# Router logits in four column groups, and class scores' products in rounds, in a ViT layer on one core

## The chip, the cores and the metric

One core of a Trainium2 chip runs the program in one launch. The metric is the device time of one execution in microseconds. The profile is of one execution; the median is of three others.

## What is computed

The input has 16 images of 512 tokens, 256 wide. The layer mixes tokens with a gated product, puts a class token ahead of each image (513 rows), adds a 16-head attention with quantized projections, and adds a mixture of 8 experts of which each token takes 2. Cut to what matters here:

```python
scores = jnp.einsum('bhqd,bhkd->bhqk', q, k) * SCALE      # 513 x 513 per head, 16 heads
attn = jax.nn.softmax(scores, axis=-1)
...
router_logits = x_flat @ gate_w                            # x_flat: layernorm(h), 8208 x 256; gate_w: 256 x 8
router_probs = jax.nn.softmax(router_logits, axis=-1)
top_k_probs, top_k_idx = jax.lax.top_k(router_probs, 2)
```

The class token's row and column of the scores are computed apart from the 512 x 512 rest: these are the "class scores". The router logits choose the experts of each token. Both are fp32 products.

## The kernel before

The token phase goes over the images in steps. One step works on five images at once, each in another stage: T (token mixing), P (projections and quantization, one image back), C (attention, the first groups of heads), W (attention, the last ones, and its output), X (output projection, second norm, router). So X's image is two behind C's, and in the last two of the 16 steps of X there is no C. Three steps ahead of the loop and the last ones are written out; between them a hardware loop runs two images a lap.

A step has 64 units (`at`), 4 groups of 16 (`u`). The order is written out by hand, for each engine in its own program, and engines meet at semaphores. In each unit:

- PE makes one tile of scores (L503) for VectorE and, with the row maximum taken in, one transposed tile (L512) for ScalarE. L503 may be only two tiles ahead of VectorE (`dve_mx`), L512 only two ahead of ScalarE (`act_exp`).
- VectorE takes the row maximum (`head_max`, L1183) at the head of the unit, then the unit's other work.
- ScalarE does the unit's other work first and `exps` (L833) last.
- Every fourth unit PE multiplies by the values (L521), four heads at once in four column groups: each product writes 32 of the bank's 128 partitions, from stationary tiles of 32 columns.

Every fp32 product with a moving tile other than a transposition shows as two records. Bank `d2` is shared in turn by many small jobs; each waits until the one before has been read.

What stands around the change, all for image X unless said:

- Unit 3 (image C): the class scores, L604 to L610. Eight products of 32 stationary and 256 moving columns, into four column groups of `d2`: for each of two operand pairs and two halves, the two slices `c` of the contraction.
- Units 28 and 30: PE transposes the normed x2 (L721); ScalarE copies it to `x2_t` in units 29 and 31 (L928).
- Unit 33: `logits` (L784 to L792). For each of four token blocks and two slices, a block of x2_t (128 columns) is the stationary operand and the 8 columns of gate_w move. The result is 128 tokens x 4 blocks x 8 experts in `d2`.
- Unit 34: VectorE copies it to `lg` (L1263), and the router goes on in units 35, 37, 41. ScalarE's unit 33 copies part_kh (L935), which waits for VectorE's fk of unit 32; unit 34 copies part_qm (L938), which releases POOL's part_ql (L1054) and then its rest (L1059).
- Unit 34 of PE also has the token product L552 (image T), unit 35 the class token's values (L748, image W) into `d2` after `dve_lg`; ScalarE's unit 36 copies pvs (L846); unit 38 of PE transposes it (L645).

A copy of `logits` serves the class tokens after the loop (L814 on). SP loads gate_w in setup (L376). The expert phase after that has nothing of the change.

Of the kernel before, what the change touches and what calls it, by code (L numbers as in the profile page):

```python
# [8 lines left out]
ACT = mybir.ActivationFunctionType  # L9
# [8 lines left out]
E, F = 8, 512  # L18
EPS = 1e-5
TB = S // 128  # L20
# [130 lines left out]
def token_phase(nc, outer, images, x_t, cls, w0_t, w1_t, wo_t, attn_w_t, gate_w, consts, out,  # L151
# [19 lines left out]

    gate_sb = keep("gate_sb", [128, DC, E])
    ones_bf = keep("ones_bf", [128, 128], BF16)
# [193 lines left out]
    def sync_program(sp, stage):  # L367
        if stage == SETUP:
            sp.dma_start(cst[:, :], consts).then_inc(s("cst_in"), 16)
            sp.dma_start(w_stage.rearrange("p (w c n) -> p w c n", w=4, c=DC),  # L370
                         attn_w_t.rearrange("w (c p) n -> p w c n", p=128)).then_inc(s("attn_w_in"), 16)
            sp.dma_start(cls_row[:, :], cls).then_inc(s("cls_in"), 16)
            sp.dma_start(w0[:, :, :], w0_t.rearrange("(c p) n -> p c n", p=128)).then_inc(s("tok_w_in"), 16)
            sp.dma_start(w1[:, :, :], w1_t.rearrange("(c p) n -> p c n", p=128)).then_inc(s("tok_w_in"), 16)
            sp.dma_start(wo[:, :, :], wo_t.rearrange("(c p) n -> p c n", p=128)).then_inc(s("tok_w_in"), 16)
            sp.dma_start(gate_sb[:, :, :], gate_w.rearrange("(c p) n -> p c n", p=128)).then_inc(s("gate_in"), 16)  # L376

# [97 lines left out]
    def tensor_program(pe, stage):  # L475
# [49 lines left out]
        def body(T, P, C, W, X):  # L525
            for g in range(NG):
                for u in range(UNITS):
# [73 lines left out]
                    if C.ok and at == 3:  # L601

                        wait(pe, s("dve_bd"), 2, C, 2)
                        wait(pe, s("act_vc"), 1, C, 1)  # L604
                        for k, (a, o) in enumerate(((fq, kbd), (fk, qbd))):
                            for half in range(2):
                                for c in range(DC):
                                    last = mm(d2[VW * (2 * k + half):VW * (2 * k + half + 1), 0:S // 2], o[:, c, :],
                                              a[:, c, half * S // 2:(half + 1) * S // 2], start=(c == 0), stop=(c == DC - 1))
                        last.then_inc(s("pe_ct"), 1)  # L610
# [99 lines left out]
                    if X.ok and at in (28, 30):  # L710
# [9 lines left out]
                        for t in range(TB):  # L720
                            last = tr(d2[:, blk(t)], x2[:, t, blk(c)], identf)  # L721
                        last.then_inc(s("pe_x2t"), 1)
                    if X.ok and at == 33:
                        logits(X, TB, 128, "", [])
                    if P.ok and at in (41, 42):
# [58 lines left out]
        def logits(b, nt, np_, x, free):  # L784
# [3 lines left out]
            for t in range(nt):  # L788
                for c in range(DC):
                    last = mm(d2[0:np_, t * E:(t + 1) * E], x2_t[:, c, t * 128:t * 128 + np_], gate_sb[:, c, :],  # L790
                              start=(c == 0), stop=(c == DC - 1))
# [29 lines left out]
    def scalar_program(act, stage):  # L821
# [13 lines left out]
        def body(T, P, C, W, X):  # L835
            for g in range(NG):
                for u in range(UNITS):
# [86 lines left out]
                    if X.ok and at in (29, 31):  # L924
                        c = (at - 29) // 2
                        wait(act, s("pe_x2t"), DC, X, c + 1)
                        wait(act, s("pe_lg"), 1, X, 0)
                        f(x2_t[:, c, :], d2[:, :], ACT.Copy).then_inc(s("act_x2t"), 1)  # L928
                    if P.ok and at == 29:
                        wait(act, s("dve_fq"), DC, P, DC)  # L930
# [165 lines left out]
    def vector_program(dve, stage):  # L1096
# [30 lines left out]
        one = At(0)  # L1127
        if stage == SETUP:
            v.memset(ones[:, :], 1.0).then_inc(s("ones_set"), 1)
            v.memset(am2[:, :], 1.0).then_inc(s("ones_set"), 1)  # L1130
# [122 lines left out]
        def router(b, x, nt, np_, pieces=(0, 1, 2, 3)):  # L1253
# [4 lines left out]
            for piece in pieces:  # L1258
                k = piece // 2
                ch = Link("dve_chain_r" + x, 10, b, (0, 2, 5, 7)[piece])  # L1260
                if piece == 0:
                    wait(dve, s("pe_lg" + x), 1, b, 1)
                    signal(v.tensor_copy(lg[P, 0:nt, :], d2[P, 0:nt * E].rearrange("p (t e) -> p t e", e=E)),  # L1263
                           "dve_lg" + x, 1, b, 1)
                if piece == 2:
# [671 lines left out]
```

## Time and profile before

| | us |
|---|---|
| median of 3 runs | 2311.74 |
| the runs | 2311.74, 2303.79, 2311.91 |
| the profiled execution | 2304.04 |
| its span, first to last instruction | 2302.2 |
| PE busy in the span | 2008.1 (87%) |
| VectorE busy | 1532.5 (67%) |
| ScalarE busy | 1266.3 (55%) |
| POOL busy | 924.0 (40%) |

"Busy" of PE is the time in which some matmul record is open; records of neighbouring matmuls overlap, since their ends are modelled. PEld is the weight load, beside PE. "Idle before" names how long the engine had done nothing ahead of an instruction, and the instruction that ended the wait. The token phase takes about the first 1650 us. In the loop an image takes 91 to 97 us.

### The profile page before, as it was taken

The page shows a single profiled execution, that of the slowest core. Times are in us where ns is not written, and L with a number is a line of the kernel's source. Part 1 is how long each engine was busy: PE and PEld are TensorE (multiplying, and loading weights), DVE is VectorE, ACT ScalarE, POOL GpSimd, SP SyncE. Part 2 cuts the span into 40 slices and gives each one's busy share as a digit, 9 for nine tenths or more (in the row PEclk, how much of TensorE's full clock was granted, in tenths as well). Part 3 has the DMA queues.
Part 4 walks back from the last instruction along what each step waited for, and adds up shares of the span by engine and source line. Part 5 has one row for each costly group of instructions (what it writes and reads, how often), then busy time and mean ns, then how long its engine had stood idle before and what let it go on. Part 6 is the DMA issues. An engine that isn't in the chain of part 4 may idle for free. (4 is left out here: it accounts for less than half of the span.)

```text
span 2302.2 us, 49649 instructions
## 1 busy us (share of the span) xinstructions
PE 2008.1 (87%) x13312; PEld 1151.8 (50%) x13329; DVE 1532.5 (67%) x4076; ACT 1266.3 (55%) x2792; POOL 924.0 (40%) x958
## 2 busy tenths in 40 slices
PE   4799999999998998989999998883139999999997
PEld 2343444443444444444344443321038898888885
DVE  4477887877877787788787888873264444444443
ACT  0246666665665665656566567662144555544553
POOL 2222233423433244233342343332236666666653
PEclk9799999999999999999899999996569999999999
DMA  2412322322232223233232322310244443333341
GB/s 85 105 56 70 95 76 78 90 79 73 84 79 85 77 68 97 67 84 87 59 97 67 89 75 79 79 43 28 96 162 66 65 64 62 61 62 62 63 59 22
DMA packets 171885, 172.29 MB, mean 75 GB/s; under 512 B 30786, under 2 KB 160404, under 8 KB 171668
## 3 DMA queue, kind: packets, MB, share of 16 engines
q1 hardware_dynamic: 141396, 134.87, 20.4%
q0 software_dynamic: 30272, 34.80, 9.5%
q8 instruction: 103, 1.69, 0.3%
q14 instruction: 114, 0.93, 0.2%
HBM read 100.70 MB, written 68.99 MB: 74 GB/s over the span
## 5 line engine op out<-in xcount | busy, mean ns | idle before, releaser
L1183 DVE TENSOR_REDUCE mxs<-bank 128x1 f32<-128x512 f32 x1024 | 698.6, 686 | 251.2 <-PE bank L503 239.4
L833 ACT ACTIVATE pt<-bank 128x512 f32<-128x512 f32 x1024 | 586.1, 592 | 277.0 <-PE bank L512 272.3
L503 PE MATMUL bank<-ks,qs 96*128 96x512 bf16 x1024 | 399.1, 391 | 72.0 <-DVE mxs L1183 53.9
L512 PE MATMUL bank<-qs,ks 99*128 99x512 bf16 x1024 | 394.7, 387 | 4.4 <-ACT pt L833 3.8
L1792 PE MATMUL bank<-xh,gu_h 128*128 128x256 bf16 (+1 forms) x1152 | 308.9, 268 | 3.8 <-issue 1.9
L1792 PE MATMUL bank<-xl,gu_h 128*128 128x256 bf16 (+1 forms) x1152 | 307.7, 267 | 0.0
L1792 PE MATMUL bank<-xh,gu_l 128*128 128x256 bf16 (+1 forms) x1152 | 307.7, 267 | 0.0
L1752 POOL DMA_INDIRECT out<-y_sb,ids x136 | 217.2, 1597 | 202.1 <-ACT y_sb L1843 177.6
L521 PE MATMUL bank<-pt,v_sb 128*32 128x512 f32 x2048 | 278.9, 617 | 0.0
L503 PEld LDWEIGHTS bank<-ks,qs 96*128 96x128 bf16 x1024 | 104.1, 102 | 338.8 <-DVE mxs L1183 212.5
L1900 DVE TENSOR_TENSOR hid_e<-bank,act_g 128x256 f32<-128x256 f32 (+1 forms) x288 | 117.1, 407 | 169.0 <-PE bank L1792 159.0
L1005 POOL DMA_INDIRECT list_dram<-pay,slot_i x130 | 138.3, 1064 | 227.0 <-DVE pay L1306 192.8
L1904 DVE TENSOR_TENSOR hl<-hid_e,hh 128x256 bf16<-128x256 f32 (+1 forms) x288 | 119.4, 415 | 143.9 <-ACT hh L1857 143.9
L1857 ACT ACTIVATE hh<-hid_e 128x256 bf16<-128x256 f32 (+1 forms) x288 | 116.5, 405 | 163.8 <-DVE hid_e L1900 163.8
L1022 POOL TENSOR_TENSOR cadd<-vcls,pr 128x256 f32<-128x256 f32 x64 | 40.9, 639 | 372.4 <-DVE pr L1228 372.1
L1742 POOL DMA_INDIRECT xg<-x_dram,ids x136 | 137.1, 1008 | 62.9 <-issue 41.2
L1803 PE MATMUL bank<-dn_h,hh 128*128 x544 | 148.5, 273 | 3.5 <-ACT hh L1857 3.5
L1803 PE MATMUL bank<-dn_h,hl 128*128 x544 | 148.3, 273 | 0.0
L1803 PE MATMUL bank<-dn_l,hh 128*128 x544 | 148.3, 273 | 0.0
L512 PEld LDWEIGHTS bank<-qs,ks 99*128 99x128 bf16 x1024 | 100.2, 98 | 90.7 <-issue 38.0
L552 PE MATMUL bank<-xt,w 128*128 128x512 f32 x256 | 130.6, 634 | 8.1 <-DMA xt<-x_t 8.0
L572 PE MATMUL bank<-wo,hid 128*128 128x256 f32 x512 | 124.1, 388 | 4.2 <-ACT v_sb L952 3.4
(290 smaller groups left out, 3432.1 us busy)
## 6 DMA issues: line engine op xcount, KB each, us to landing
qs<-qk_dram SPq DMA_DIRECT2D x128, 128.0 KB, 2.6
ks<-qk_dram SPq DMA_DIRECT2D x64, 192.0 KB, 3.3
xt<-x_t SPq DMA_DIRECT2D x16, 512.0 KB, 4.4
h_dram<-h_sb SPq DMA_DIRECT2D x16, 512.0 KB, 4.1
qs<-qk_dram SPq DMA_DIRECT2D x128, 64.0 KB, 2.2
ks<-qk_dram SPq DMA_DIRECT2D x64, 128.0 KB, 3.3
hw<-h_dram SPq DMA_DIRECT2D x16, 512.0 KB, 4.1
out<-hw SPq DMA_DIRECT2D x16, 512.0 KB, 3.0
```

The costliest lines, as they stand in the source:

```text
L503: mm(score[u % 2][:, :], qs[0:QK, h, blk(t)], ks[0:QK, h, :], start=True, stop=True) \
L512: mm(scoret[u % 2][:, :], ks[0:QK + MROWS, h, blk(t)], qs[0:QK + MROWS, h, :], start=True, stop=True).then_inc(s("pe_st"), 1)
L521: last = mm(pv_bank[VW * j:VW * (j + 1), :], v_sb[:, b.par, t, g * GH + j, :], pt[:, t % 2, j, :], start=(t == 0), stop=(t == TB - 1))
L552: last = mm(d0[:, :], w0[:, c, blk(e)], xt[:, T.par, c, :], start=(c == 0), stop=(c == DC - 1))
L572: last = mm((d0, d1)[t // 2][:, D * (t % 2):D * (t % 2 + 1)], hid[:, e, blk(t)], wo[:, e, :], start=(e == 0), stop=(e == EC - 1))
L833: f(pt[:, t % 2, j, :], scoret[u % 2][:, :], ACT.Exp).then_inc(s("act_exp"), 1)
L1005: g_.indirect_dma_start(out=list_dram, out_offset=bass.IndirectOffsetOnAxis(ap=slot_i[0:np_, k, t:t + 1], axis=0), in_=pay[0:np_, k, t, :] ...
L1183: v.reduce_max(mxs[:, t, g * GH + j:g * GH + j + 1], score[u % 2][:, :], AX.X).then_inc(s("dve_mx"), 1)
L1742: nc.gpsimd.indirect_dma_start(out=xg[:, i.place(ROWS), b, :], out_offset=None, in_=x2_dram, in_offset=rows(i, b)) \
L1752: nc.gpsimd.indirect_dma_start(out=out, out_offset=rows(i, b), in_=y_sb[:, i.place(2), b, :], in_offset=None, bounds_check=tokens - 1, oob ...
L1792: last = mm(bank[:, 0:n], w[:, bass.ds(e, 1), c, lo:lo + 128], a[:, k, c, 0:n], start=(m == 1), stop=(m == 3 * DC))
L1803: last = mm(y_b[b][:, 0:D], a[:, c, blk(b)], w[:, bass.ds(e, 1), c, :], start=(c == 0 and m == 0), stop=(c == FC - 1 and m == 2))
```

## The change

The class scores' eight products are issued in another order: the slice `c` outermost, so that four products to four column groups follow one another. The router logits of the 16 images are made the other way round: gate_w, padded to 32 columns with zeros, is stationary, the token block moves, and each token block has its own column group; they move to unit 32. They come out transposed (32 padded experts x 4 blocks by 128 tokens), so ScalarE copies them to a new tile `lgt` in its unit 32, PE transposes that in unit 33, and VectorE reads the result from the second quarter of `d2`. The zeros are set by VectorE in setup, and SP's load of gate_w waits for them.

```diff
-    gate_sb = keep("gate_sb", [128, DC, E])
+    gate_sb = keep("gate_sb", [128, DC, VW])
+    lgt = keep("lgt", [128, 128])
...
-            sp.dma_start(gate_sb[:, :, :], gate_w.rearrange("(c p) n -> p c n", p=128)).then_inc(s("gate_in"), 16)
+            sp.wait_ge(s("gate_set"), 1)
+            sp.dma_start(gate_sb[:, :, 0:E], gate_w.rearrange("(c p) n -> p c n", p=128)).then_inc(s("gate_in"), 16)
...
-                        for k, (a, o) in enumerate(((fq, kbd), (fk, qbd))):
-                            for half in range(2):
-                                for c in range(DC):
+                        for c in range(DC):
+                            for k, (a, o) in enumerate(((fq, kbd), (fk, qbd))):
+                                for half in range(2):
                                     last = mm(d2[VW * (2 * k + half):VW * (2 * k + half + 1), 0:S // 2], o[:, c, :],
                                               a[:, c, half * S // 2:(half + 1) * S // 2], start=(c == 0), stop=(c == DC - 1))
...
+                    if X.ok and at == 32:
+                        wait(pe, s("act_x2t"), DC, X, DC)
+                        for c in range(DC):
+                            for t in range(TB):
+                                last = mm(d2[VW * t:VW * (t + 1), 0:128], gate_sb[:, c, :], x2_t[:, c, blk(t)],
+                                          start=(c == 0), stop=(c == DC - 1))
+                        last.then_inc(s("pe_lgt"), 1)
                     if X.ok and at == 33:
-                        logits(X, TB, 128, "", [])
+                        wait(pe, s("act_lgt"), 1, X, 1)
+                        tr(d2[:, 128:256], lgt[:, :], identf).then_inc(s("pe_lg"), 1)
...
-                    last = mm(d2[0:np_, t * E:(t + 1) * E], x2_t[:, c, t * 128:t * 128 + np_], gate_sb[:, c, :],
+                    last = mm(d2[0:np_, t * E:(t + 1) * E], x2_t[:, c, t * 128:t * 128 + np_], gate_sb[:, c, 0:E],
...
+                    if X.ok and at == 32:
+                        wait(act, s("pe_lgt"), 1, X, 1)
+                        wait(act, s("pe_lg"), 1, X, 0)
+                        f(lgt[:, :], d2[:, 0:128], ACT.Copy).then_inc(s("act_lgt"), 1)
...
+            v.memset(gate_sb[:, :, :], 0.0).then_inc(s("gate_set"), 1)
...
-                    signal(v.tensor_copy(lg[P, 0:nt, :], d2[P, 0:nt * E].rearrange("p (t e) -> p t e", e=E)),
-                           "dve_lg" + x, 1, b, 1)
+                    got = d2[P, 0:nt * E].rearrange("p (t e) -> p t e", e=E) if x else \
+                        d2[:, 128:256].rearrange("p (t w) -> p t w", w=VW)[:, :, 0:E]
+                    signal(v.tensor_copy(lg[P, 0:nt, :], got), "dve_lg" + x, 1, b, 1)
```

## Rows read from the trace of the kernel before

**Rows 1.** The profile page, its head.

```profile
span 2302.2 us, 49649 instructions
```

**Rows 2.** Stretch between two logits: its length, busy us of PE, PEld, DVE, ACT, POOL.

```profile
968.71:1061.40 92.69, 85.79 (x482) 38.56 (x483) 74.31 (x203) 57.81 (x124) 34.02 (x42) 0.98 0.28 77
```

**Rows 3.** Timeline of PE, units 32 to 34: start us, length us, engine, line.

```profile
966.35 0.38 PE L512 MATMUL bank<-qs,ks 99*128 99x512 bf16 x1
966.57 0.38 PE L503 MATMUL bank<-ks,qs 96*128 96x512 bf16 x1
...
967.00 1.85 PE L790 MATMUL bank<-gate_sb,x_t 128*128 128x8 f32 x16
968.71 0.38 PE L503 MATMUL bank<-ks,qs 96*128 96x512 bf16 x1
...
969.14 0.59 PE L552 MATMUL bank<-xt,w 128*128 128x512 f32 x1
```

**Rows 4.** Groups by line: busy us, mean ns; of L895 min/median/max ns.

```profile
L790 PEld LDWEIGHTS bank<-gate_sb,x_t 128*128 128x128 f32 x260 | 32.8, 199 | 4.4 <-ACT x_t L928 1.9 <-ACT x_t L976 0.4
L608 PEld LDWEIGHTS bank<-fq,kbd 128*32 128x32 f32 x128 | 8.0, 116 | 14.8 <-DVE qbd L1357 11.2 <-issue 2.1
L645 PEld LDWEIGHTS bank<-cst,pvs 128*128 128x128 f32 x256 | 31.8, 141 | 11.9 <-issue 1.7
...
L895 ACT ACTIVATE sct<-bank x16: 372/381/391, 107.3 to 1474.4; 128x256 f32<-128x256 f32 x16
```

**Rows 5.** Timelines of ACT, then of DVE, units 31 to 37.

```profile
964.85 0.59 ACT L928 ACTIVATE x_t<-bank 128x512 f32<-128x512 f32 x1
...
966.85 0.60 ACT L833 ACTIVATE pt<-bank 128x512 f32<-128x512 f32 x1
967.93 1.06 ACT L935 ACTIVATE part_kh<-fk 128x1024 bf16<-128x1024 f32 x1 [0.48 <-DVE fk L1450]
...
972.60 0.60 ACT L846 ACTIVATE pvs<-bank 128x512 f32<-128x512 f32 x1 [0.28 <-PE bank L521]
...
969.12 0.69 DVE L1183 TENSOR_REDUCE mxs<-bank 128x1 f32<-128x512 f32 x1 [0.46 <-PE bank L503]
...
976.58 0.69 DVE L1183 TENSOR_REDUCE mxs<-bank 128x1 f32<-128x512 f32 x1 [1.00 <-PE bank L503]
```

**Rows 6.** Timeline of PE at the class scores of the same step, unit 3.

```profile
924.99 0.41 PE L608 MATMUL bank<-fq,kbd 128*32 128x256 f32 x2
925.00 0.42 PE L608 MATMUL bank<-fk,qbd 128*32 128x256 f32 x2
925.20 0.41 PE L608 MATMUL bank<-fq,kbd 128*32 128x256 f32 x2
...
925.68 0.39 PE L608 MATMUL bank<-fk,qbd 128*32 128x256 f32 x2
926.00 0.39 PE L503 MATMUL bank<-ks,qs 96*128 96x512 bf16 x1
```

**Rows 7.** Timeline of PE at the products with the values, unit 35.

```profile
971.08 0.38 PE L512 MATMUL bank<-qs,ks 99*128 99x512 bf16 x1
971.38 1.06 PE L521 MATMUL bank<-pt,v_sb 128*32 128x512 f32 x8
```

**Rows 8.** Timeline of PE and DVE, units 38 to 40.

```profile
977.03 0.60 PE L645 MATMUL bank<-cst,pvs 128*128 128x128 f32 x4
977.47 0.38 PE L503 MATMUL bank<-ks,qs 96*128 96x512 bf16 x1
...
979.21 0.68 DVE L1183 TENSOR_REDUCE mxs<-bank 128x1 f32<-128x512 f32 x1
...
979.95 0.39 PE L503 MATMUL bank<-ks,qs 96*128 96x512 bf16 x1 [0.35 <-DVE mxs L1183]
```

**Rows 9.** Timeline of POOL, the first work behind its chain of part_ql and rest.

```profile
981.76 0.63 POOL L1022 TENSOR_TENSOR cadd<-vcls,pr 128x256 f32<-128x256 f32 x1 [6.33 <-DVE pr L1228]
```

**Rows 10.** Timeline of PE in the last image's step.

```profile
1615.06 3.58 PE L790 MATMUL bank<-gate_sb,x_t 128*128 128x8 f32 x16 [0.69 <-ACT x_t L928]
```

## The prediction

> **What bounds the kernel now.** I read the page's head first, then the table of stages, then stretches in order of time. The span is 2302.2 us [rows 1]; the profiled execution took 2304.04 us, so 1.8 us lie around the span. A whole stretch from one image's logits to the next shows PE busy 85.79 of 92.69 us (93%), VectorE 80%, ScalarE 62% [rows 2]. PE is the engine to relieve. It is not the only limit: in some units it waits for VectorE's maxima, as at 979.95 [rows 8]. So I ask of each saving whether PE sets the end where it falls, and what comes next.
>
> The old logits (L790) are a plain stop of PE. From their first product at 967.00 to the next scores (L503) at 968.71 pass 1.71 us [rows 3]. Weight loads fill them: 16 loads of 128 fp32 columns, 199 ns each and overlapping by half (260 in all: 16 for each of 16 images, 4 in the class-token stage) [rows 4], against products of 8 columns. In 14 of the 16 steps another image's scores stand beside them (that image is two ahead). Meanwhile VectorE waits: 0.46 us before the maximum at 969.12 and 1.00 before that at 976.58, both for L503 [rows 5]. The first wait of PE behind the logits is the 0.35 us at 979.95 [rows 8]. Hence VectorE follows PE here, and time saved at the logits starts everything behind it earlier.
>
> **The class scores' order costs or gives nearly nothing.** The edit only changes the order of 8 products (16 records, since each is two passes). The four column groups already run side by side: records of both pairs start at 924.99 and 925.00, the next round at 925.20 [rows 6]. The last round ends its starts at 925.68 and the next scores start at 926.00, so 1.01 us in all, against 4 rounds of 0.21 = 0.85 plus the way out. Rounds in the program can remove only the stagger inside a round, about 0.02 us: 16 x 0.02 = 0.3 us. Bounds: 0 and 1.01 - 0.85 = 0.16 us an image.
>
> [...]
>
> **The logits, step by step**, on the clock of [rows 3] (the old start is 967.00).
> 1. In unit 32 the L512 product starts at 966.35 and its neighbour 0.22 later, so PE is free at 966.57. Entering column groups costs 0.09 us: L521 starts 0.30 after L512 at 971.38, where 0.21 is usual [rows 7]. First logit product: 966.66. The wait for x2_t is over: its second copy ended at 965.44 [rows 5] (964.85 + 0.59).
> 2. Eight fp32 products in four groups are 16 records, 4 rounds. A round of 256 columns takes 0.21 us [rows 6]; 128 columns I take at half, 0.107. End 967.09. The way out costs 0.11 (925.68 + 0.21 to 926.00) [rows 6], so unit 33's L503 starts at 967.20, L512 at 967.42, PE free at 967.63.
> 3. ScalarE's new copy waits for those products. Its nearest relation: L846 starts at 972.60, 0.16 after the modelled end of the L521 group, 971.38 + 1.06 [rows 5, 7]. The new group's modelled end is its last start 966.98 + 0.27 = 967.25 (L608's records last 0.17 longer than their round). Copy starts at 967.41. Copies of 256 and 512 columns last 381 and about 600 ns [rows 4, 5]; 128 columns: 0.27 us. End 967.68.
> 4. PE's transposition waits for it, 0.06 us after (L503 starts at 979.95 after the maximum that ended at 979.21 + 0.68) [rows 8]. Four transpositions take 977.03 to 977.47, 0.11 each [rows 8]; a weight load not made ahead adds up to 0.14 (141 ns) [rows 4]. PE free at 967.99, after a stall of 0.11 + 0.14.
> 5. exps(32) is queued behind the copy on ScalarE: it ran at 966.85, now at 967.66 to 968.26. PE's scoret of unit 34 needs it: L512 at 968.32 instead of 968.21. The token product L552 then starts at 968.54 instead of 969.14 [rows 3].
>
> Saving: **0.60 us an image**. Bounds: 1.71 - 0.09 - 0.43 - 0.11 - 0.11 = 0.97 if copy and weight load hide; 0.60 - 0.45 = 0.15 if each round also waits for its loads (0.11 each, L608's load records [rows 4]). No trace row shows 128-column rounds, so both ends stay.
>
> [...]
>
> **Who is behind the new waits.** Behind ScalarE's copy stand exps(32), the copy of part_kh, exps(33), part_qm and relu. part_kh waited for VectorE's fk until 967.93 anyway [rows 5], so this queue runs about 0.3 us later up to exps(35), at 972.0. PE needs exps(34) only in unit 36, over 2 us later, and pvs waited 0.28 us for PE until 972.60 before [rows 5]: the delay ends there. POOL's part_ql, released by part_qm, moves 0.3 us later, but POOL is idle 6.33 us behind that chain [rows 9]. VectorE's router copy (L1263) at 969.73 waits for the transposition, ready at about 968.2 and so covered by the maximum before it. SP gets one wait in setup, on VectorE's first instruction; PE waits there for other loads and weights: 0. The added memset: 0.
>
> From unit 36 on nothing crosses the saving: the waits of [rows 8] are VectorE's own work since its last wait for PE (976.58), which starts earlier as well. They stay as long as they were. So 14 x 0.60 = 8.4 us.
>
> **The last image** runs its logits alone, at the lower clock level: L790 lasts 3.58 us from 1615.06, and VectorE has nothing else to do [rows 10]. The new chain: 4 rounds at twice the time 0.86, ScalarE 0.29 + 0.27, transposition 0.06 + 0.28, way to VectorE 0.2 = 1.96 us; gain 1.6. The image before it has PE waiting for ScalarE's exps at several places; I take 0. The class-token stage keeps its old products (0).
>
> Sum: 8.4 + 1.6 + 0.3 = 10.3, rounded to 10 us: 2304.0 - 10 = 2294.0 on the profiled execution's scale. The median shown is 2311.7, 7.7 us above that execution, two runs near 2311.8 and one at 2303.8. Shifted by that, the forecast is **2301.7 us**, a gain of 0.43%. About 0.5%, 11.5 us, is what a measurement of this kernel can tell from no change.
>
> **Rivals.**
> - Everything hidden. For it: ScalarE is idle 0.48 us before part_kh, and PE could keep loading ahead. Against: PE's unit 33 holds just 0.43 us of work between the products and the transposition, the copy chain 0.65. Price 0.97 x 14 + 1.6 + 0.3 = 15.5 us: 2296 us. Chance 0.17.
> - Rounds wait for their loads. For it: 16 loads and 16 products now stand against 0.43 us of streaming, where L608 has 0.85. Price 0.15 x 14 + 1 = 3 us: 2309 us. Chance 0.16.
> - Slower: **the four groups don't overlap** on short products. Place: unit 32. All 16 records one after another take 16 x 0.107 = 1.71 us, as long as the old ones, and entry, exit, stall (0.25) and transposition (0.11) come on top; exps(32) is 1.3 us later again and holds PE's unit 34 by 0.1 to 0.3 more. Together about +0.8 us x 14 = +11: 2323 us. It decides once a round takes above 0.107 + 0.60/4 = 0.26 us. Against it: L608 groups overlap wholly [rows 6]. Chance 0.12.
> - The class scores gain more: if a group's second record could not start before its first and held up the other groups, the old order would take 4 groups x 3 rounds x 0.21 + 0.21 = 2.7 us, and the new one 1.0: 1.7 x 14 = 24 us more, 2278 us. The measured 1.01 excludes it [rows 6]; chance under 0.01, counted in the first rival.
> - That the change does nothing (column groups not used) is the same as the slower case.
>
> **How the numbers follow.** Forecast case 0.55: range 7 to 13 us of gain, 2298.7 to 2304.7; 0.17 of it lies beyond 11.5 us. Faster by over 0.5%: 0.17 + 0.17 = 0.34. Slower by over 0.5%: 0.10 of the slower rival's 0.12. Within: 0.56. The range goes from the full relief with the median sitting 5 us lower than I shifted it, 2291, to the small gain with 2 us for the unknown bound, 2311. It leaves out the slower rival and some edges, under 0.2.
>
> **What would show it.** Right: L608 from first record to next L503 stays 1.0 us; the new products fill about 0.43 us in unit 32; L512 of unit 32 to L552 of unit 34 is about 2.2 us (was 2.79); a short PE stall before the transposition; L833 at unit 32 about 0.8 us later; VectorE's idle at 969.12 shrinks; the time between logits of neighbouring images falls by 0.6 us. Wrong: a round over 0.2 us, a stall over 0.5 us before the transposition, or step lengths that don't follow, because a wait between 976 and the next logits grew.

## The result, and the profile after

| | before | changed |
|---|---|---|
| median of 6 runs each, us | 2305.5 (2302.1 to 2311.9) | 2290.65 (2285.2 to 2295.9) |
| ratio of the two, with its 95% interval | | 0.9927 (0.9904 to 0.995) |
| profiled execution, us | 2304.04 | 2290.1 |

The medians differ by 14.9 us, where 10 was forecast; the ratio of the comparison gives 0.73%. The changed kernel's 2290.65 us lie 0.35 us below the range and 11.05 us below the forecast of 2301.7. On the profiled executions the gain is 13.9 us. Medians here and below leave out two executions of the kernel before, which took 3231 and 5119 us.

The head of the page and its first table, changed kernel:

```profile
span 2288.3 us, 49749 instructions
...
PE 1996.3 (87%) x13344; PEld 1124.2 (49%) x13345; DVE 1526.2 (67%) x4077; ACT 1265.1 (55%) x2808; POOL 926.0 (40%) x958
```

PE's busy time falls by 11.8 us and ScalarE's is the same in spite of 16 new copies. Now the stretch between two logits that answers to [rows 2], from the same score of one image to that of the next (length, then busy us of PE, PEld, VectorE, ScalarE, POOL; the granted clock is the third from the end):

```profile
961.24:1053.21 91.97, 85.50 (x503) 37.53 (x499) 75.36 (x209) 58.83 (x125) 34.14 (x42) 1.00 0.28 82
```

It is 0.72 us shorter. Units 32 to 34 of that image on PE, to be laid beside [rows 3]:

```profile
960.35 0.38 PE L514 MATMUL bank<-qs,ks 99*128 99x512 bf16 x1
960.66 0.64 PE L729 MATMUL bank<-x_t,gate_sb 128*32 128x128 f32 x16
961.24 0.39 PE L505 MATMUL bank<-ks,qs 96*128 96x512 bf16 x1
961.47 0.38 PE L514 MATMUL bank<-qs,ks 99*128 99x512 bf16 x1
961.78 0.33 PE L734 MATMUL bank<-cst,lgt 128*128 128x128 f32 x1
961.95 0.38 PE L505 MATMUL bank<-ks,qs 96*128 96x512 bf16 x1
962.30 0.39 PE L514 MATMUL bank<-qs,ks 99*128 99x512 bf16 x1
962.52 1.53 PE L554 MATMUL bank<-xt,w 128*128 128x512 f32 x3
```

L729 are the new products and L734 the transposition; the other lines are those of before, moved down by two (L503 is L505, L512 is L514, L521 is L523, L552 is L554). From the transposed scores ("scoret", L514) of unit 32 to the token product of unit 34 are 2.17 us, where 2.79 were. ScalarE and VectorE beside it, for [rows 5] (L942 is the new copy, L843 the exps, L949 the copy of part_kh, L1198 the maximum):

```profile
961.45 0.28 ACT L942 ACTIVATE lgt<-bank 128x128 f32<-128x128 f32 x1 [0.68 <-PE bank L729]
961.64 0.60 ACT L843 ACTIVATE pt<-bank 128x512 f32<-128x512 f32 x1
962.14 1.05 ACT L949 ACTIVATE part_kh<-fk 128x1024 bf16<-128x1024 f32 x1
...
962.59 0.68 DVE L1198 TENSOR_REDUCE mxs<-bank 128x1 f32<-128x512 f32 x1
```

ScalarE's idle time before part_kh is gone, and the maximum after the logits no longer waits for PE (0.46 us before).

**Where the time went.** Read from the starts of PE's scores, the 14 images of each profile in which the loop's order holds (C's images 2 to 15) split into stretches. Each row of this table is the sum of one stretch over these images, worked out as the difference of the starts of two scores, so the columns add up to the span (the row 62 to the next image's 5 holds that image's class scores). The last two columns are the ranges over four profiles of each kind: before, again_before, rounds_only and one_more_memset; after, again_after, joint_after and logits_only.

| stretch (units) | before | changed | difference | kind of before | kind with the logits |
|---|---|---|---|---|---|
| start, to unit 28 of image 2 | 303.1 | 303.6 | +0.5 | 302.4 to 307.1 | 303.2 to 304.0 |
| 28 to 36, the logits | 177.4 | 170.1 | -7.3 | 177.4 to 177.4 | 169.9 to 170.4 |
| 36 to 41 | 80.3 | 80.3 | 0.0 | 80.3 to 80.3 | 80.3 to 80.3 |
| 41 to 46 | 99.8 | 99.1 | -0.7 | 99.8 to 103.2 | 99.1 to 102.0 |
| 46 to 48 | 57.4 | 52.9 | -4.5 | 52.9 to 58.7 | 52.9 to 56.2 |
| 48 to 62 | 234.0 | 232.4 | -1.6 | 232.5 to 234.0 | 232.4 to 233.6 |
| 62 to the next image's 5 | 141.9 | 143.0 | +1.1 | 141.9 to 146.0 | 140.0 to 148.0 |
| 5 to 28 | 427.0 | 426.6 | -0.4 | 426.6 to 427.0 | 425.8 to 427.6 |
| end, from unit 48 of image 15 | 781.2 | 780.3 | -0.9 | 781.2 to 784.3 | 780.3 to 781.6 |

Only the second row lies apart in all profiles of the two kinds, and it holds what was forecast: 7.3 us for 8.4. The saving is not the same in every image: 0.54 us in images 3 to 12 (0.38 in one of them), 0.72 in images 2 and 13, 0.67 in image 15, and in image 14 the stretch is 0.09 longer. The next largest term, 4.5 us in units 46 to 48, is one that the forecast did not have. Four rows (41 to 46, 46 to 48, 48 to 62, and the lap's end, 62 to 5) take several values in one and the same kernel; the lap's end moves most, by 8 us between profiles of the kind with the logits. The means of the four profiles of each kind differ by 13.4 us: 7.3 for the logits, 2.2 in units 46 to 48, 1.5 in units 41 to 46, 1.6 at the end, the rest small.

**Units 46 to 48.** Before, PE there, image 9 (L572 is the output projection):

```profile
988.26 0.61 PE L503 MATMUL bank<-ks,qs 96*128 96x512 bf16 x1 [0.58 <-DVE mxs L1183]
988.66 0.63 PE L512 MATMUL bank<-qs,ks 99*128 99x512 bf16 x1
989.09 3.19 PE L572 MATMUL bank<-wo,hid 128*128 128x256 f32 x8
```

and in the changed kernel:

```profile
981.50 0.39 PE L505 MATMUL bank<-ks,qs 96*128 96x512 bf16 x1 [0.58 <-DVE mxs L1198]
981.73 0.38 PE L514 MATMUL bank<-qs,ks 99*128 99x512 bf16 x1
981.95 1.89 PE L574 MATMUL bank<-wo,hid 128*128 128x256 f32 x8
```

The same products behind the same wait, at another clock. The stretches of 5 us say so; the third number from the end is the granted clock. Before:

```profile
985.00:990.00 5.00, 3.52 (x17) 2.05 (x18) 4.42 (x12) 2.17 (x4) 0.53 (x1) 0.83 0.53 167
```

Changed:

```profile
977.00:982.00 5.00, 3.23 (x23) 1.20 (x20) 4.81 (x10) 2.54 (x6) 2.00 (x2) 1.00 0.39 116
```

Such a spell of the lower clock (granted clock 0.50 from 988.3 to 991.5 us) costs 1.6 us here (5.5 where 3.9 is usual). The profile of before has it at images 7 and 9, and one of 1.3 us at image 14; that of the changed kernel has none in these units. Another one of before, also in image 14 (granted clock 0.66 in the stretch from 1455 to 1460 us), is 1.3 of the 1.6 us in the row 48 to 62.

**Units 41 to 46.** Six units in which VectorE makes the last part of the router. Most even images take 6.6 us there; odd ones 6.6 or 8.3 before, 6.6 or 8.1 after. VectorE in an image with 8.3, before, and beside it POOL, which follows its L1022 of [rows 9] with L1026:

```profile
981.78 0.66 DVE L1275 SCALAR_TENSOR_TENSOR rtmp<-rtmp,cst 128x32 f32<-128x32 f32 x1
982.47 0.19 DVE L1276 TENSOR_REDUCE ix<-rtmp 128x4 f32<-128x32 f32 x1
982.69 0.65 DVE L1277 TENSOR_TENSOR oh<-cst,ix 128x32 f32<-128x32 f32 x1
983.38 1.08 DVE L1280 TENSOR_TENSOR picked<-oh 128x32 bf16<-128x32 f32 x1
...
984.99 0.56 DVE L1289 TENSOR_SCALAR wts<-e21e 128x4 f32<-128x4 f32 x1
...
982.57 0.73 POOL L1026 TENSOR_TENSOR o_sb<-o_sb,cadd 128x256 f32<-128x256 f32 x1 [0.18 <-POOL cadd L1022]
```

and the three with two inputs in an image with 6.6, before:

```profile
415.23 0.18 DVE L1275 SCALAR_TENSOR_TENSOR rtmp<-rtmp,cst 128x32 f32<-128x32 f32 x1
...
415.67 0.29 DVE L1277 TENSOR_TENSOR oh<-cst,ix 128x32 f32<-128x32 f32 x1
415.99 0.19 DVE L1280 TENSOR_TENSOR picked<-oh 128x32 bf16<-128x32 f32 x1
```

The three with two SBUF inputs take two to six times as long. Of those with one input the reduction L1276 keeps its 0.19 us, but L1289 takes 0.56 where it takes 0.16 in the short image. The slow ones don't just run slower: each ends 0.03 to 0.05 us after the POOL operation beside it. L1275 ends at 982.44 and POOL's L1022 at 982.39, L1277 at 983.35 and L1026 at 983.30, and L1280 and L1289 end so behind the two L1064 that follow. So a slow one seems to wait POOL's operation out; the traces show the ends, the cause is not tested. Of the five odd images between the third and the eleventh, three are long in the profile of before, three in that of the changed kernel, four in again_after and joint_after, five in again_before, rounds_only, one_more_memset and logits_only. The second difference, 8.3 against 8.1, is a wait of VectorE for its own L1290, which the trace of before has five times (us, times), though it holds PE only in the three long images:

```profile
L1291 DVE TENSOR_TENSOR wts<-e21e,wts x13: 161/604/848, 327.3 to 1442.4; 128x4 f32<-128x4 f32 x13
...
  DVE wts L1290: 1.4, 5
```

In the changed kernel the same instruction (L1307) has no such line.

**The last image**, for [rows 10]:

```profile
1603.64 1.08 PE L729 MATMUL bank<-x_t,gate_sb 128*32 128x128 f32 x16 [0.69 <-ACT x_t L938]
...
1604.79 0.28 ACT L942 ACTIVATE lgt<-bank 128x128 f32<-128x128 f32 x1 [1.20 <-PE bank L729]
...
1605.12 0.48 PE L734 MATMUL bank<-cst,lgt 128*128 128x128 f32 x1 [0.40 <-ACT lgt L942]
1605.63 0.19 DVE L1280 COPY lg<-bank 128x32 f32<-128x32 f32 x1 [7.75 <-PE bank L734]
```

PE's 16 records take 1.08 us for 3.58 before, both at a granted clock of 0.50.

**The class scores**, for [rows 6]: rounds now stand evenly, and the whole is 0.04 us shorter (0.98 from the first record to the next scores, for 1.01).

```profile
919.04 0.39 PE L610 MATMUL bank<-fq,kbd 128*32 128x256 f32 x2
919.05 0.39 PE L610 MATMUL bank<-fk,qbd 128*32 128x256 f32 x2
919.26 0.39 PE L610 MATMUL bank<-fq,kbd 128*32 128x256 f32 x2
...
920.02 0.39 PE L505 MATMUL bank<-ks,qs 96*128 96x512 bf16 x1
```

### The profile page after: what moved, and what is told of

It is laid out like the page before. It is cut to its first block and busy times, and to the rows that moved or that the text cites. A ratio compares the mean times of both kernels' runs of the same rounds, so it can differ in the third digit from the quotient of the medians.

```text
span 2288.3 us, 49749 instructions
## 1 busy us (share of the span) xinstructions
PE 1996.3 (87%) x13344; PEld 1124.2 (49%) x13345; DVE 1526.2 (67%) x4077; ACT 1265.1 (55%) x2808; POOL 926.0 (40%) x958
## 5 line engine op out<-in xcount | busy, mean ns | idle before, releaser
L1198 DVE TENSOR_REDUCE mxs<-bank 128x1 f32<-128x512 f32 x1024 | 698.0, 685 | 245.3 <-PE bank L505 233.9
L843 ACT ACTIVATE pt<-bank 128x512 f32<-128x512 f32 x1024 | 586.7, 593 | 264.4 <-PE bank L514 260.4
L505 PE MATMUL bank<-ks,qs 96*128 96x512 bf16 x1024 | 397.6, 389 | 72.1 <-DVE mxs L1198 54.1
L514 PE MATMUL bank<-qs,ks 99*128 99x512 bf16 x1024 | 393.9, 386 | 5.7 <-ACT pt L843 5.1
L1808 PE MATMUL bank<-xh,gu_h 128*128 128x256 bf16 (+1 forms) x1152 | 309.4, 269 | 3.6 <-issue 2.0
L1808 PE MATMUL bank<-xl,gu_h 128*128 128x256 bf16 (+1 forms) x1152 | 308.2, 268 | 0.0
L1808 PE MATMUL bank<-xh,gu_l 128*128 128x256 bf16 (+1 forms) x1152 | 308.1, 267 | 0.0
L523 PE MATMUL bank<-pt,v_sb 128*32 128x512 f32 x2048 | 278.7, 617 | 0.0
L505 PEld LDWEIGHTS bank<-ks,qs 96*128 96x128 bf16 x1024 | 103.1, 101 | 340.0 <-DVE mxs L1198 218.3
L514 PEld LDWEIGHTS bank<-qs,ks 99*128 99x128 bf16 x1024 | 100.2, 98 | 95.6 <-issue 39.0
L554 PE MATMUL bank<-xt,w 128*128 128x512 f32 x256 | 130.4, 633 | 8.4 <-DMA xt<-x_t 7.9
```

Of the source, the lines that this page charges most:

```text
L505: mm(score[u % 2][:, :], qs[0:QK, h, blk(t)], ks[0:QK, h, :], start=True, stop=True) \
L514: mm(scoret[u % 2][:, :], ks[0:QK + MROWS, h, blk(t)], qs[0:QK + MROWS, h, :], start=True, stop=True).then_inc(s("pe_st"), 1)
L523: last = mm(pv_bank[VW * j:VW * (j + 1), :], v_sb[:, b.par, t, g * GH + j, :], pt[:, t % 2, j, :], start=(t == 0), stop=(t == TB - 1))
L554: last = mm(d0[:, :], w0[:, c, blk(e)], xt[:, T.par, c, :], start=(c == 0), stop=(c == DC - 1))
L843: f(pt[:, t % 2, j, :], scoret[u % 2][:, :], ACT.Exp).then_inc(s("act_exp"), 1)
L1198: v.reduce_max(mxs[:, t, g * GH + j:g * GH + j + 1], score[u % 2][:, :], AX.X).then_inc(s("dve_mx"), 1)
```

## The experiments

Each ratio is to runs of the kernel before on the same chip, with its 95% interval. "28 to 36" is the length of that stretch, from score to score, in most images of the loop: 12.99 us before, 12.44 changed. Some images of a profile take 0.15 more.

### Which part of the change carries it

**rounds_only**: the kernel before with the class scores' loops in the new order, nothing else.

```diff
-                        for k, (a, o) in enumerate(((fq, kbd), (fk, qbd))):
-                            for half in range(2):
-                                for c in range(DC):
+                        for c in range(DC):
+                            for k, (a, o) in enumerate(((fq, kbd), (fk, qbd))):
+                                for half in range(2):
```

> The kernel before with the class scores' products in rounds, logits as before. Theory A: from the first class score record to the next scores 0.979 us instead of 1.016, so 0.04 us x 14 = 0.5 us, no difference that can be measured: ratio 1.000. Rival: the order gives a part of the 4.6 us by which the gain of 14.9 us exceeds the 10.3 forecast; then this kernel is 3 to 5 us faster than the kernel before.

Measured: 2309.5 us, ratio 0.9997 (0.9984 to 1.0011); 28 to 36 is 12.99. **logits_only**: the changed kernel with the class scores' old order, the same lines turned back.

> The changed kernel with the class scores' old order. Theory A: all of the gain is here: ratio 0.993 to 0.994, 2290 to 2292 us, class score stretch back at 1.016 us. Rival: 3 to 5 us slower than the changed kernel, ratio 0.995.

Measured: 2298.0 us, 0.9942 (0.992 to 0.9965); 12.44. Beside them the two kernels themselves, **again_before**

> The kernel before, unchanged, against itself. Theory A: part of the difference between two executions comes from where spells of the lower clock (granted clock 0.5 of full) fall, and these fall differently in each execution of one and the same kernel. Then the ratio is 1.000 with an interval of about +-0.002, single times scatter over 2302 to 2312 us, and the new profile shows the lower clock at unit 46 of other images than 7 and 9. Theory B: the spells belong to the program. Then the same images 7 and 9 lose 1.6 us each again, and the step lengths repeat to 0.1 us.

with 2310.1 us, 1.001 (0.9997 to 1.0022), and **again_after**

> The changed kernel, unchanged. Theory A: ratio 0.993 to 0.995; L514 of unit 32 to L554 of unit 34 again 2.17 us in all 14 images, while the lead over the kernel before grows by another amount in steps with a different count of low clock spells. Theory B: every step length of the first profile (90.5, 94.9, 92.0, 95.7, 92.0 us and so on) repeats to 0.1 us.

with 2296.3 us, 0.9936 (0.9917 to 0.9955). The whole gain comes with the logits; that of the class scores is not to be told from 0 (0.04 us x 16 = 0.6 us by the trace). Of the theories on the repeats, neither holds as written: again_before has the spells at images 3, 7 and 9 and five long images, where before had 7 and 9 and three. The places are those of the program, but whether one comes at a place changes between executions. On this chip both kernels are slower by about 5 us than where the result was taken, and the gain is 14.0 us.

### Do the column groups overlap, and does their order matter

**group_major** issues the new products group by group:

```diff
-                        for c in range(DC):
-                            for t in range(TB):
+                        for t in range(TB):
+                            for c in range(DC):
```

> The changed kernel with the eight logit products in the old order: both slices of a token block, then the next block. Theory A (the column groups take their work side by side whatever the order in the program): first logit record to next scores 0.58 to 0.65 us instead of 0.576, time as the changed kernel, ratio 0.992 to 0.996. Rival (starts are bound to the program's order, rounds matter on short products): 4 blocks x 3 further passes x 0.107 = 1.4 us instead of 0.576, 12 us slower, ratio 0.999.

Measured: 2299.3 us, 0.9944 (0.9923 to 0.9965); 28 to 36 is 12.50. The products fill 0.59 us to the next scores instead of 0.58, and the copy comes 0.05 later:

```profile
968.18 0.66 PE L729 MATMUL bank<-x_t,gate_sb 128*32 128x128 f32 x16
968.77 0.39 PE L505 MATMUL bank<-ks,qs 96*128 96x512 bf16 x1
```

So the order of issue hardly matters: four groups run side by side either way, with the short products too. The rival (1.4 us) is refuted.

**one_group** gives all four blocks the same column group, so that nothing can overlap; ScalarE copies 32 rows of 512, and PE makes four transpositions. The blocks go out one after the other, and VectorE's setup has one more memset (of `lgt`) with a wait for it, which is left out here:

```diff
-                                last = mm(d2[VW * t:VW * (t + 1), 0:128], ...
+                                last = mm(d2[0:VW, blk(t)], ...
...
-                        tr(d2[:, 128:256], lgt[:, :], identf).then_inc(s("pe_lg"), 1)
+                        for t in range(TB):
+                            last = tr(d2[:, blk(t)], lgt[:, blk(t)], identf)
+                        last.then_inc(s("pe_lg"), 1)
```

> The changed kernel with all eight products into one column group, the blocks side by side in the bank; the copy is 32 x 512 and four transpositions follow. Theory A: nothing overlaps, 16 records x 0.107 = 1.7 us in unit 32; copy 0.6 instead of 0.28 us, transpositions 0.43 instead of 0.11. L514 of unit 32 to L554 of unit 34 about 4.0 us instead of 2.17: +1.8 us an image, ratio 1.003 to 1.006. It prices the slower rival of the prediction. Rival: products of 32 stationary columns in one group are not slower than in four, then unit 32 stays near 0.6 us and only copy and transpositions add 0.6 us an image, ratio 0.998.

Measured: 2350.0 us, 1.0178 (1.0158 to 1.0197); 28 to 36 is 14.13, which is 1.69 more than changed and 1.14 more than before.

```profile
975.77 1.94 PE L729 MATMUL bank<-x_t,gate_sb 128*32 128x128 f32 x16
977.64 0.39 PE L505 MATMUL bank<-ks,qs 96*128 96x512 bf16 x1
...
978.46 0.55 PE L735 MATMUL bank<-cst,lgt 128*128 128x128 f32 x3 [0.21 <-ACT lgt L944]
```

16 records one after another take 1.87 us to the next scores: this is the slower rival at work. It does not explain the whole time. The stretches give 23.5 us more for the logits than in the changed kernel and 31 more at the end, after unit 48 of the last image (811.3 against 780.3). In the expert phase PE's products stood still five times, for 3.9 to 4.7 us each; with the line of the changed kernel (L1808) first, of this one (L1812) second:

```profile
L1808 PE MATMUL bank<-xh,gu_h 128*128 128x256 bf16 (+1 forms) x1152 | 309.4, 269 | 3.6 <-issue 2.0 <-DVE xl L1907 1.6
```

```profile
L1812 PE MATMUL bank<-xh,gu_h 128*128 128x256 bf16 (+1 forms) x1152 | 313.3, 272 | 23.1 <-issue 21.3 <-DVE xl L1911 1.6
```

PE waits 21.3 us for nothing that the profile shows, in a phase whose code the edit does not change, though the edit moves its place in the program. Its cause is open, and about 12 us of the 31 are not accounted for; the verdict on the rival rests on the stretch of units 28 to 36 alone, where 1.8 us more were expected and 1.69 came. The ratio expected (1.003 to 1.006) failed by this phase.

### What the new chain over ScalarE costs

**copy_twice** makes ScalarE's copy a second time, into a tile that nobody reads.

```diff
+                        f(lgt2[:, :], d2[:, 0:128], ACT.Copy)
                         f(lgt[:, :], d2[:, 0:128], ACT.Copy).then_inc(s("act_lgt"), 1)
```

> The changed kernel with ScalarE's copy of the logits made twice (the first into a spare tile), 0.2 to 0.28 us more ahead of the transposition and of exps(32). Theory A (the copy chain stands open on PE): L514 of unit 32 to L554 of unit 34 grows by the whole 0.2 to 0.28 us, +3 to +4 us in all, ratio 0.995. Rival (the chain is hidden, PE's stall comes from elsewhere): no change in that stretch, ratio 0.9935.

Measured: 2297.4 us, 0.9945 (0.9929 to 0.996); 28 to 36 is 12.59, 0.15 more for a copy that takes 0.18 from the start of one to that of the next. The chain from products over copy to transposition sets the time nearly one for one: the transposition moves from 1.12 to 1.29 us after the first product. **at31** takes the products to unit 31, one unit earlier, and leaves the transposition where it is:

```diff
-                    if X.ok and at == 32:
+                    if X.ok and at == 31:
```

> The changed kernel with the eight logit products in unit 31, behind the products with the values, which are in column groups already; copy and transposition stay in units 32 and 33. Theory A: one entry and one exit (0.09 and 0.11 us) and the stall of the transposition (0.10 us) go, and exps(32) is 0.5 us earlier: 0.3 to 0.4 us less an image, 4 to 6 us in all, ratio 0.991. Rival: unit 31 waits for ScalarE's second copy of x2_t, or exps(31) and the maximum of unit 32 take over the wait, and nothing is gained: ratio 0.9935.

Measured: 2291.0 us, 0.9914 (0.99 to 0.9927); 28 to 36 is 12.10, another 0.34 less.

```profile
959.05 1.06 PE L523 MATMUL bank<-pt,v_sb 128*32 128x512 f32 x8
959.94 0.62 PE L729 MATMUL bank<-x_t,gate_sb 128*32 128x128 f32 x16
960.49 0.39 PE L505 MATMUL bank<-ks,qs 96*128 96x512 bf16 x1
...
961.16 0.38 PE L514 MATMUL bank<-qs,ks 99*128 99x512 bf16 x1
961.37 0.27 PE L734 MATMUL bank<-cst,lgt 128*128 128x128 f32 x1
961.67 0.39 PE L505 MATMUL bank<-ks,qs 96*128 96x512 bf16 x1
```

Unit 31 ends with the products with the values, which are in column groups already. From the first of them (L523) to the scores behind the logits' products pass 1.44 us. In the changed kernel they take 0.99 to the next scores, and the logits' products 0.58 and 0.09 ahead of them (0.31 after L514, where 0.22 is usual): 1.66 together. So the way in and out is there once for both, and the transposition stands 0.21 after L514: no stall.

**late_tr** leaves the products in unit 32 and takes the transposition to unit 34; **at31_tr32** has products in 31 and transposition in 32.

```diff
-                    if X.ok and at == 33:
+                    if X.ok and at == 34:
```

> The changed kernel with the transposition of the logits in unit 34 instead of 33. Theory A: the 0.10 us stall ahead of it goes, but L514 of unit 34 still waits for exps(32), so units 28 to 36 take 12.35 to 12.44 us instead of 12.44: nothing measurable, ratio 0.9935. Rival: the copy back to VectorE now comes too late for the router piece of unit 34 and VectorE holds PE in unit 36: up to 0.4 us an image more, ratio 0.996.

Measured: 2292.4 us, 0.9967 (0.9951 to 0.9984), 28 to 36 is 12.56, which is 0.12 more than changed, where no difference was expected. PE's stall before the transposition is replaced by one before the scoret, behind exps(32):

```profile
970.01 0.38 PE L505 MATMUL bank<-ks,qs 96*128 96x512 bf16 x1
970.62 0.39 PE L514 MATMUL bank<-qs,ks 99*128 99x512 bf16 x1 [0.23 <-ACT pt L843]
```

> Products in unit 31 and the transposition in unit 32. Theory A: ScalarE's copy in unit 32 stands behind nmp, which waits for VectorE's last maximum; with the transposition in unit 32 PE waits for it, 0.4 to 0.5 us an image lost against at31, ratio 0.994. Rival: the copy is early enough, ratio as at31, 0.9914.

Measured: 2289.6 us, 0.9942 (0.9925 to 0.9959), 28 to 36 is 12.10, as at31. The expectation that the transposition would wait and lose fell: the wait is there, 0.1 us, but the next scores follow the transposition after 0.17 us, where they follow it after 0.30 in at31, and the stretch comes out equal. These two ran on another chip than at31, and the changed kernel did not run on it, so their ratios are not to be held against those above; the stretches are.

### The terms beside the logits

**one_more_memset** adds nothing but one small memset to VectorE's setup in the kernel before, so that all its later instructions lie one further on:

```diff
+            v.memset(lg[:, :, :], 0.0).then_inc(s("lg_set"), 1)
             v.memset(ones[:, :], 1.0).then_inc(s("ones_set"), 1)
```

> The kernel before with one more memset in VectorE's setup (of lg, 128 x 32), as the change has one. Theory E: the wait of 0.27 us before L1291 in five images of the kernel before, which no version with the change shows, hangs on where the instructions of VectorE's program lie, not on the logits. Then it is gone here, units 41 to 46 take 8.07 us in the images with a collision instead of 8.32, and the time falls by about 1 us (ratio 0.9995). Rival: it comes from the logits' place; then 8.32 us stay.

Measured: 2307.5 us, 0.9988 (0.9976 to 1.0), 1.6 us less than the kernel before by medians, with an interval that reaches 1.0; the traces are clearer. The wait before wts is gone, and long odd images take 8.08 us in units 41 to 46, not 8.32. Even images take 18.18 in units 48 to 62 for 18.26, as in the changed kernel. The changed kernel has an added memset as well. This part of its gain has nothing to do with the logits: 3 long images x 0.24 and 5 even ones x 0.07, 1.1 us in the profiles of the result. That it is the place of the instructions which counts, and not something else about the memset, is not shown.

**router38** and **router38_at31** try to move VectorE's two-input work from the place where POOL is busy: the last part of the router from unit 41 to 38 and the weights from 42 to 40, in the changed kernel and in at31.

```diff
-ROUTER_AT = (34, 35, 37, 41)
+ROUTER_AT = (34, 35, 37, 38)
...
-                    if X.ok and at == 42:
+                    if X.ok and at == 40:
```

> The changed kernel with the router's last piece moved from unit 41 to 38 and the weights from unit 42 to 40, ahead of POOL's work of units 41 and 42. Theory C: the step from unit 41 to 46 takes 8.07 us in most odd images and 6.62 in the others because small VectorE operations with two inputs in SBUF (0.18 us) last 0.65 to 1.08 us beside a POOL operation; away from POOL they last 0.18 and all images take 6.0 to 6.6 us there, against up to 0.8 us more at units 38 to 40: 4 to 8 us less in all, ratio 0.990 to 0.992. Rival: VectorE's total work sets these units, moving it gains nothing, ratio 0.9935.

> Both: the logit products in unit 31, and the router's last piece and the weights ahead of POOL's work. Theory: the two gains lie in different units and add, ratio 0.988 to 0.990 (2282 to 2287 us). Rival: the earlier router piece delays unit 39 and 40 for PE by as much as it saves later, then it stays at at31's 0.9914.

Measured: 2295.5 us, 0.9976 (0.9959 to 0.9993), and 2294.0 us, 0.9972 (0.9958 to 0.9987). Both theories failed in the time. The operations themselves did what was expected: away from POOL they last 0.18 to 0.19 us. But PE waits for the maximum that stands behind them, and then for o_sb (router38, image 9):

```profile
976.72 0.39 PE L505 MATMUL bank<-ks,qs 96*128 96x512 bf16 x1 [1.12 <-DVE mxs L1198]
...
978.01 0.59 PE L659 MATMUL bank<-id_bf,nmp 128*12 128x128 bf16 x4 [0.68 <-DVE o_sb L1242]
...
979.36 0.63 PE L505 MATMUL bank<-ks,qs 96*128 96x512 bf16 x1
```

Units 36 to 41 took 91.1 us over the 14 images for 80.3. Behind these two waits PE has the lower clock (granted clock 0.50 from 978.5 to 981 us; the score at 979.36 lasts 0.63 us for 0.39). Such a spell comes in eight images of router38 and seven of router38_at31; with it units 41 to 46 take 7.5 to 7.7 us, without it most take 6.0 to 6.1. It does not come behind every such pair of waits: the same 1.12 and 0.68 us at 411.98 and 1168.47 us of router38 have a granted clock of 1.00 behind them. The spells ate most of what was gained in units 41 to 46: the 14 images sum to 99.6 and 98.1 us for the 102 of at31. On that chip the kernel before ran at 2302.5, and one and the same kernel, at31_tr32, had the ratio 0.9942 there and 0.991 in the comparison below.

### The three versions side by side

On one chip, the kernel before at 2309.1 us (14 runs):

> The changed kernel again, on the chip of the next two. Theory D (the clean part of the gain is fixed, the rest is chance and chip): u28 to u36 again 12.44 us; ratio between 0.9927 and 0.997.

> Products of the logits in unit 31. u28 to u36 12.10 us; 0.35 x 13 = 4.5 us less than joint_after, ratio lower by 0.002. Rival: the lower clock and the collisions give it back, the same as joint_after.

> Products in unit 31, transposition in unit 32. Its u28 to u36 was 12.10 us too, so the transposition did not wait as I had expected: the same as joint_at31 within 0.001.

| | median, us | ratio | 28 to 36 |
|---|---|---|---|
| joint_after, the changed kernel | 2297.3 | 0.9947 (0.9933 to 0.9961) | 12.45 |
| joint_at31 | 2291.0 | 0.9912 (0.9896 to 0.9928) | 12.10 |
| joint_at31_tr32 | 2289.4 | 0.991 (0.9895 to 0.9926) | 12.10 |

Both versions beat the changed kernel, by 6 to 8 us. In the profiles the stretch itself gives 4.0 us for joint_at31 and 2.2 for joint_at31_tr32, less than 0.34 x 14 = 4.8: images 2 and 13 save only 0.23, and image 14 takes longer by 0.34 and 1.9. The rest goes the way of the side terms.

## Why the prediction was wrong, and where it was right

**The logits' chain, step by step, held.** First product 0.31 us after the scoret (forecast 0.30); 0.58 from it to the next scores (0.54); the copy starts 0.79 after the first product and takes 0.28 (0.75 and 0.27); scoret to token product is 2.17 us ("about 2.2"). One number was off: transposition and the wait before it. The stall is 0.10 (0.11), but the load of the transposition was not paid on top: 0.17 us to the next scores where 0.25 was forecast. So 0.62 us were gained up to the token product of unit 34. From there to the next scores pass 1.80 us for 1.72 before, so that by unit 36 most images have gained 0.54 us, not 0.60: 7.3 us over 14 images for 8.4. The ends of the bound both fell: copy_twice shows that the copy does not hide, and the products do not wait for their loads (256 of them, 0.11 us each, in 0.58 us for 16).

**Who waits behind the copy** held: exps(32) starts 0.98 us after the first product, the order of ScalarE closes up before part_kh, and units 36 to 41 are unchanged to 0.1 us in all profiles of the table. **The last image** held: from ScalarE's last copy of x2_t to VectorE's copy of the logits the lead over the kernel before grows from 11.42 to 13.05 us, 1.6 as forecast; the row of the end shows 0.9, since 0.7 go again in the expert phase. **The class scores**: 0.04 us an image for 0.02.

**The step that failed most is the anchor,** the shift of 7.7 us from the profiled execution to the median. Of three runs two lay near 2311.8; six runs have their median only 1.5 us above the profiled execution. That is 6.2 of the 11.05 us by which the forecast was too high. With the right shift it would have been 2295.5.

**The second is the gain, 10 us for 14.9,** which makes up the other 4.9. Its step is "from unit 36 on nothing crosses the saving", with "the added memset: 0": all that follows was taken as 0. The table shows -6.8 us from units 41 to 62. Of these 1.1 are what an added memset does by itself (one_more_memset), so that 0 was wrong. The other 5.7 are the spells at images 7, 9 and 14 that the profile of before has and that of the changed kernel has not; the long images number three in both. These spells are not tied to the kind: rounds_only and logits_only have none in units 46 to 48, one_more_memset has two, again_before three and a part of a fourth, again_after one and joint_after two. The saving of PE stayed, as argued. Whether the change makes spells rarer is open.

The terms of the change that repeat sum to 7.3 + 1.1 + 1.6 + 0.6 = 10.6 us, near the 10.3 of the forecast. The comparisons gave more: 14.9 in the result, 14.0 with again_after, 11.8 with joint_after. So the sum was near for the repeating part, partly by luck, since the logits were put 1.1 us too high and the memset 1.1 too low; and the excess of the result is in part that of its executions. In the last comparison the mean clocks were equal (0.9510 changed, 0.9507 before); in the result the changed kernel's was 0.9542. Within one kernel a run is about 1.1 us shorter for 0.001 more of clock (slope over the runs of all kernels, each against its own mean; correlation -0.56).

**The rivals.** Slower, groups that don't overlap: refuted by the changed kernel and group_major, and its price was right in kind; one_group shows +1.14 us an image over before where 0.8 was worked out. Rounds that wait for loads: refuted. Everything hidden: its time, 2296 by the same shifted median, is the nearest of those forecast, but not its mechanism; the stall and the order behind the copy are there, and at31 shows that 0.34 us of it were still to be had. The class scores gain more, since one group holds up the others: refuted by rounds_only and group_major. Rows 6 refute more than the waiting. In the kernel before all eight records of the first pair stand ahead of the second pair's in the program, yet the second pair's records start at 925.00 and the first pair's third at 925.20. So the records start in rounds over the column groups, whatever the order in the program, and this is why the order of issue is worth almost nothing.

## What to carry to other kernels

Here the fp32 products with few moving columns cost as much as their weight loads (16 records of 8 columns in 1.71 us, beside 16 loads of 199 ns that overlap by half); turned round, with the narrow operand stationary and each block in a column group of its own, 1.7 us became 0.6, and a copy, a transposition and a stall took back about half of that saving. Put such products right beside others that are in column groups already: that gave another 0.34 us on top of 0.54. Before moving small work to a place where another engine is quiet, ask which wait it lengthens there: in router38 eight images also had a spell at a granted clock of 0.50 behind the longer waits (1.12 and 0.68 us), though at 411.98 and 1168.47 us the same waits had none. For a gain under 1% count what repeats (here one stretch, same in every profile) apart from what takes several values in the same kernel, and don't move a forecast by the median of three runs.

## What the runs showed of the hardware that was not expected

- Small VectorE operations with two SBUF inputs last 0.65 to 1.09 us beside work of POOL, until 0.05 us after POOL's operation ends, and 0.18 to 0.19 away from it. It need not happen: with POOL's L1022 beside L1275 in both images (from 415.21 on in the short one) it came once and not the other time, though POOL starts 0.02 us ahead in both. What decides is open. It is not bound to two inputs either: L1289, with one, took 0.56 us where it takes 0.16, while the reduction L1276 kept its 0.19. The price is 1.45 us an image (8.07 for 6.62), and 1.7 with the wait for L1290.
- Records of fp32 products in different column groups start in rounds over the groups and not in the order of the program (925.00 against 925.20 in rows 6).
- One memset more in VectorE's setup takes away 0.27 us of waiting between two neighbours hundreds of us later, in each of five images.
- A spell at a granted clock of 0.50 comes in some executions and not in others, at the same place of the same program, behind the same pause of PE of 0.58 us: the granted clock is 1.00 behind the one before 793.68 us in the changed kernel and 0.50 behind the same one, before 798.07 us, in again_after.
- 16 records of 128 fp32 columns take 1.87 us to the next scores in one column group and 0.58 in four, the way out with it in both.
- In one_group the expert phase had 21.3 us of waits at issue, in five pieces, for 2.0 in the changed kernel, also in five, with no edit there.
